# A four-stage transformer block: the second feed-forward with its scales behind the magnitudes, three parts a tile and half-word integers

## The reference

```python
def bit_linear(x, w, g):
    xn = rms_norm(x, g)                       # g: a weight for each column
    scale = 127.0 / clip(max(abs(xn)), 1e-05) # one for each row
    xq = clip(round(xn * scale), -128, 127) / scale
    wq = ...                                  # weights to -1, 0, 1 times one scale
    return xq @ wq.T
y = bit_linear(layernorm(x), gate_w, gate_norm_w)  # 512 -> 2 x 1408
gate, up = split(y, 2)
h = gate * sigmoid(gate) * up
x = x + tanh(g_ffn[1]) * bit_linear(h, down_w, down_norm_w)  # 1408 -> 512
```

## Time and profile before

| | us |
|---|---|
| median of 3 runs (lowest, highest) | 890.92 (889.18, 891.5) |
| the profiled execution | 892.4 |
| its span, first to last instruction | 890.6 |
| TensorE busy | 677.7 (76%) |
| VectorE busy | 681.8 (77%) |
| ScalarE busy | 607.0 (68%) |
| GpSimd busy | 325.4 (37%) |
| granted TensorE clock, mean | 0.90 |
| ScalarE's one table load in `ffn1` (L2106) | 1.28 |
| GpSimd's `integers` over 1408 columns (L2061), mean | 1.44 |

### The profile page before, as it was taken

How to read it: one execution, slowest core, us unless ns; L and a number is a source line. 1 busy time by engine, 2 the same in 40 slices (tenths; PEclk the granted TensorE clock), 3 DMA queues, 4 the chain that set the end, 5 groups by cost and what they waited for, 6 DMA issues and landing times. The chain is left out here.

```text
span 890.6 us, 14235 instructions
## 1 busy us (share of the span) xinstructions
PE 677.7 (76%) x5231; PEld 373.6 (42%) x5262; DVE 681.8 (77%) x1144; ACT 607.0 (68%) x812; POOL 325.4 (37%) x357
## 2 busy tenths in 40 slices
PE   5863367867576856779999988899998377979796
PEld 2431123333233324446555554566455144535453
DVE  1689999999999995886874796556342588989984
ACT  2688698989949883688863885589271155757574
POOL 0113514525685563463561274113031023333233
PEclk9986586998879878689999999999999698989899
DMA  8900300000000002422320121123000000000001
GB/s 317 340 0 0 119 23 1 1 1 1 1 1 1 1 0 99 130 83 70 108 78 1 34 66 45 38 68 106 1 1 1 33 1 12 25 24 24 24 36 48
DMA packets 21760, 43.70 MB, mean 49 GB/s; under 512 B 3904, under 2 KB 8512, under 8 KB 20800
## 3 DMA queue, kind: packets, MB, share of 16 engines
q1 hardware_dynamic: 21696, 42.85, 13.9%
HBM read 38.61 MB, written 4.19 MB: 48 GB/s over the span
## 5 line engine op out<-in xcount | busy, mean ns | idle before, releaser
L1539 DVE TENSOR_REDUCE c_nmax<-c_s 128x1 f32<-128x384 f32 (+3 forms) x176 | 108.6, 633 | 83.3 <-PE c_s L1749 83.3
L1651 ACT ACTIVATE c_probs<-c_e 128x512 f32<-128x512 f32 (+1 forms) x176 | 94.4, 558 | 56.5 <-PE c_e L1779 55.3
L1247 PE MATMUL b_y<-w2q,b_q2T 128*128 128x512 bf16 x254 | 76.6, 457 | 55.7 <-ACT b_q2T L1164 28.1
L1474 POOL TENSOR_TENSOR c_psum<-c_probs 128x1536 f32<-128x1536 f32 x16 | 55.9, 3493 | 155.8 <-ACT c_probs L1651 155.8
L2177 PE MATMUL d_gu<-gateq,d_xqT 128*128 128x352 bf16 x512 | 95.0, 336 | 13.4 <-DVE d_h L1978 12.4
L1746 PE MATMUL c_s<-c_kT,c_qaT 96*128 96x128 f16 (+3 forms) x256 | 73.3, 319 | 22.0 <-DVE c_nmax L1539 19.6
L1777 PE MATMUL c_e<-c_qaT,c_kT 98*128 98x512 f16 (+3 forms) x256 | 69.8, 307 | 4.0 <-ACT c_qaT L1638 3.8
L2106 ACT ACTIVATE d_sg<-d_gu,d_dq 128x352 f32<-128x352 f32 x64 | 35.3, 553 | 54.1 <-PE d_gu L2177 54.1
L1218 PE MATMUL b_up<-shared,b_xqT 128*128 128x512 bf16 x242 | 68.3, 402 | 4.0 <-ACT hidden L1130 2.8
L2177 PEld LDWEIGHTS d_gu<-gateq,d_xqT 128*128 128x128 bf16 x512 | 49.9, 103 | 50.0 <-DVE d_h L1978 18.3
L1247 PEld LDWEIGHTS b_y<-w2q,b_q2T 128*128 128x128 bf16 x256 | 26.5, 111 | 97.1 <-issue 50.0
(11 more groups left out here) (237 smaller groups left out, 1814.6 us busy)
## 6 DMA issues: line engine op xcount, KB each, us to landing
c_stage<-in_gateT SPq DMA_DIRECT2D x16, 704.0 KB, 4.0
c_stage<-in_downT SPq DMA_DIRECT2D x6, 768.0 KB, 4.7
xs<-in_x SPq DMA_DIRECT2D x4, 1024.0 KB, 17.5
a_w1f<-in_w1T SPq DMA_DIRECT2D x2, 2048.0 KB, 16.2
hidden<-in_w2T SPq DMA_DIRECT2D x2, 2048.0 KB, 20.8
out<-xs SPq DMA_DIRECT2D x16, 256.0 KB, 2.0
a_ctxT<-in_ctxT SPq DMA_DIRECT2D x1, 1024.0 KB, 4.9
b_ln_g<-in_ln_g SPq DMA_DIRECT2D x1, 1024.0 KB, 4.8
```

The source lines that it names most:

```text
L1247: last = nc.tensor.matmul(y_ps[:], q2T[:, n % 2, c, :], w2q[:, c, :], start=(c == 0), stop=(c == IC - 1))
L1474: nc.gpsimd.tensor_tensor(psum[:], region(slot, 0)[:, :, P:], region(slot, 1), ALU.add).then_inc(psum_ready, 1)
L1539: nc.vector.tensor_reduce(nmax[:, G % 2, i, n:n + heads], s_ps[u % 2][:, 0:heads * (i + 1) * P].rearrange("p (n k) -> p n k", n=heads), ax ...
L1651: nc.scalar.activation(probs[:, G % 2, at:at + width], e_ps[fill % 3][:, 0:width], ACT.Exp).then_inc(e_read, 1)
```

## The change

- Input quantisation moves to a class `GateInputs`. VectorE centres and weighs the raw tile (`weighted`), takes its maximum (`largest`); the scales are made behind that on GpSimd (`scales`, five operations on one column); ScalarE rounds in place, with the magic number plus 256 (`integers`), so that the low half word of each value is an integer that TensorE transposes as it is. Statistics are taken tile by tile.
- The hidden values go the same way: `weighted` multiplies by `dw` without waiting for the squares, `largest` follows, GpSimd makes all scales in one chain, ScalarE rounds in place; GpSimd's pass over 1408 columns is gone. The copies out of PSUM read 16-bit integers and take 256 off.
- The gate and up columns are in three parts (512, 512, 384) and not four of 352. `u` has three slots, `q2T` two. A tile is turned while tile `n + 2` goes up, and multiplied down in the turn of tile `n + 3`.
- The first two tiles' inputs are made inside `xattn1`: VectorE at units 189 and 190, GpSimd from 189 to 191, ScalarE at 192 and 193. `dw` gets a wait of its own, in front of `weighted(0)`.
- The hardware loops are gone: all 16 tiles are written out on all engines.

Leading parts of the diff; removed functions are those printed above:

```diff
+class GateInputs:
+    SLOTS = 2
...
+        self.bn, self.mv, self.xn = g["prep"].bn, g["prep"].mv, g["prep"].turned
...
+    def weighted(self, dve, n):
...
+        last = self.small.mark(nc.vector.bn_stats(self.bn[:, i, :], self.xs[:, n, :]))
+        dve.wait_ge(self.step, last)
+        last = self.small.mark(nc.vector.bn_aggr(self.mv[:, i, :], self.bn[:, i, :]))
+        dve.wait_ge(self.step, last)
+        nc.vector.tensor_scalar(self.ve[:, c], self.mv[:, i, 1:2], 1.0 + self.EPS, self.EPS * self.EPS,
+                                ALU.mult, ALU.add).then_inc(self.ve_ready, 1)
+        if n >= self.SLOTS:
+            dve.wait_ge(self.xqt_done, n - self.SLOTS + 1)
+        self.small.mark(nc.vector.scalar_tensor_tensor(out=self.xn[:, n % self.SLOTS, :], in0=self.xs[:, n, :], scalar=self.mv[:, i, 0:1],
+                                                       in1=self.gw[:], op0=ALU.subtract, op1=ALU.mult))
+    def largest(self, dve, n):
...
+        self.nc.vector.tensor_reduce(self.mx[:, n:n + 1], self.xn[:, n % self.SLOTS, :], axis=AX, op=ALU.max,
+                                     apply_absolute_value=True).then_inc(self.mx_ready, 1)
+    def scales(self, pool, n):
...
+        last = self.chain.mark(nc.gpsimd.tensor_tensor(self.c1[:, c], self.ve[:, c], self.minus_half[:, 0:1], ALU.pow))
+        pool.wait_ge(self.pstep, last)
+        pool.wait_ge(self.mx_ready, n + 1)
+        last = self.chain.mark(nc.gpsimd.tensor_scalar(self.e[:, c], self.mx[:, c], self.c1[:, c], 1e-5, ALU.mult, ALU.max))
+        pool.wait_ge(self.pstep, last)
+        last = self.chain.mark(nc.gpsimd.tensor_tensor(self.inv[:, c], self.e[:, c], self.minus_one, ALU.pow))
+        self.chain.mark(nc.gpsimd.tensor_scalar(self.dq[:, c], self.e[:, c], self.step_scale, 1.0, ALU.mult, ALU.mult))
+        pool.wait_ge(self.pstep, self.chain.value())
+        nc.gpsimd.tensor_scalar(self.qs[:, c], self.inv[:, c], self.c1[:, c], QMAX, ALU.mult, ALU.mult).then_inc(self.qs_ready, 1)
+    def integers(self, act, n):
...
+        act.wait_ge(self.qs_ready, n + 1)
+        at = self.xn[:, n % self.SLOTS, :]
+        self.nc.scalar.activation(at, at, ACT.Copy, scale=self.qs[:, n:n + 1], bias=MAGIC + LIFT).then_inc(self.rounded, 1)
...
+    INPUTS_AT = UNITS + LAG - 2
...
+                if u == INPUTS_AT:
+                    pool.wait_ge(w_scale_ready, 2)
+                    inputs.setup(pool)
+                if INPUTS_AT < u <= INPUTS_AT + 2:
+                    inputs.scales(pool, u - INPUTS_AT - 1)
...
+                if u == INPUTS_AT:
+                    dve.wait_ge(y_read, 2)
+                    dve.wait_ge(g["vec1_loaded"], 16)
+                if INPUTS_AT <= u < INPUTS_AT + 2:
+                    inputs.weighted(dve, u - INPUTS_AT)
+                    inputs.largest(dve, u - INPUTS_AT)
...
+                if INPUTS_AT + 3 <= u < INPUTS_AT + 5:
+                    inputs.integers(act, u - INPUTS_AT - 3)
...
+    WIDTHS = (DIM, DIM, INTER - 2 * DIM)
...
         def _(dve):
+            for n in range(TOTAL + 3):
+                gated(n, 0)
+                largest(n - 1)
+                gated(n, 1)
+                residual(n - 3)
+                inputs.weighted(dve, n + 2)
+                inputs.largest(dve, n + 2)
+                gated(n, 2)
+                weighted(n)
...
         def _(pool):
+            for n in range(TOTAL + 1):
+                scales(n - 1)
+                inputs.scales(pool, n + 2)
...
         def _(act):
+            gather(0)
+            for n in range(TOTAL + 2):
+                silu(n, 0)
+                if n >= 1:
+                    inputs.integers(act, n + 1)
+                squares(n - 1)
+                silu(n, 1)
+                gather2(n - 2, 0)
+                gather(n + 1)
+                silu(n, 2)
+                gather2(n - 2, 1)
+                integers(n - 1)
...
         def _(pe):
+            turn_inputs(0)
+            for n in range(TOTAL + 3):
+                up(n, 0)
+                down(n - 3)
+                turn_hidden(n - 2, 0)
+                up(n, 1)
+                turn_hidden(n - 2, 1)
+                turn_inputs(n + 1)
+                up(n, 2)
```

More of the change, by code:

```diff
@@ L1972, in gated @@
-            def gated(n, i, k):
+                part = n * PARTS + k
+                if n >= 2 and k == 0:
+                    dve.wait_ge(ssq_ready, n - 1)
+                    dve.wait_ge(u_ready, n - 1)
+                dve.wait_ge(sg_ready, part + 1)
+                nc.vector.scalar_tensor_tensor(out=h[:, n % 2, STARTS[k]:STARTS[k] + WIDTHS[k]], in0=gu_ps[part % 2][:, 1, 0:WIDTHS[k]],
+                                               scalar=inputs.dq[:, n:n + 1], in1=sg[:, part % 2, 0:WIDTHS[k]],
+                                               op0=ALU.mult, op1=ALU.mult).then_inc(h_ready, 1)
@@ L1999, in residual, with _, scales @@
+        @block.gpsimd
+        def _(pool):
+            chain = Tally(pstep)
+            def scales(n):
                 if not valid(n):
                     return
[L2001 to L2020 removed]
@@ L2022, in _ @@
-            nc.vector.memset(minus_one[:], -1.0).then_inc(setup, 1)
-            nc.vector.tensor_scalar(scale2[:], w1_scale[:, 1:2], gate4[:, 3:4], None, ALU.mult).then_inc(setup, 1)
-            dve.wait_ge(vec_loaded, 32)
-            statistics(0)
-            quantise(0, 0, 0)
-            batch(0)
-            with dve.Fori(1, BATCH - 1) as b:
-                small.enter(b - 1, 8 + TILES * 7)
-                batch(b)
-                small.leave(BATCH - 2)
-            batch(BATCH - 1)
@@ L2079, in _ @@
-            pool.wait_ge(setup, 2)
-            inputs_scale(0)
-            batch(0)
-            with pool.Fori(1, BATCH - 1) as b:
-                small.enter(b - 1, TILES * 3)
-                batch(b)
-                small.leave(BATCH - 2)
-            batch(BATCH - 1)
-            batch(BATCH)
-        @block.scalar
-        def _(act):
-            def gather(n, i):
-                if not valid(n):
-                    return
-                act.wait_ge(xqt_done, n + 1)
-                if past(n, 2):
+                act.wait_ge(inputs.xqt_done, n + 1)
@@ L2156, in turn_inputs @@
                 if not valid(n):
                     return
-                pe.wait_ge(xq_ready, n + 1)
-                if past(n, 1):
+                pe.wait_ge(inputs.rounded, n + 1)
+                if n >= 1:
                     pe.wait_ge(xqT_ready, n)
+                rows = low(inputs.xn[:, n % inputs.SLOTS, :])
                 for c in range(CH):
-                    last = nc.tensor.transpose(t1_ps[:, c * P:(c + 1) * P], xq[:, i % 2, c * P:(c + 1) * P], ident_b[:])
-                last.then_inc(xqt_done, 1)
@@ L2165, in up @@
-            def up(n, i, parts):
+                    last = nc.tensor.transpose(t1_ps[:, c * P:(c + 1) * P], rows[:, c * P:(c + 1) * P], ident_b[:])
+                last.then_inc(inputs.xqt_done, 1)
+            def up(n, k):
                 if not valid(n):
                     return
-                if parts[0] == 0:
+                part = n * PARTS + k
+                if k == 0:
                     pe.wait_ge(xqT_ready, n + 1)
-                for k in parts:
-                    part = n * PARTS + k
-                    if not isinstance(part, int) or part >= 2:
-                        pe.wait_ge(h_ready, part - 1)
-                    for half in range(2):
-                        at = half * INTER + k * PART
-                        for c in range(CH):
-                            last = nc.tensor.matmul(gu_ps[k % 2][:, half, 0:PART], xqT[:, i % 2, c, :],
-                                                    gateq[:, c, at:at + PART], start=(c == 0), stop=(c == CH - 1))
-                    last.then_inc(gu_done, 1)
@@ L2181, in turn_hidden @@
-            def turn_hidden(n, i):
+                if part >= 2:
+                    pe.wait_ge(h_ready, part - 1)
+                for half in range(2):
+                    at = half * INTER + STARTS[k]
+                    for c in range(CH):
+                        last = nc.tensor.matmul(gu_ps[part % 2][:, half, 0:WIDTHS[k]], xqT[:, n % 2, c, :],
+                                                gateq[:, c, at:at + WIDTHS[k]], start=(c == 0), stop=(c == CH - 1))
+                last.then_inc(gu_done, 1)
```

324 lines of the change are left out of this document (128 added, 196 removed).

## The result

The changed kernel takes **856.88 us** (median of 4 runs, 856.03 to 858.79) against 890.64 for the kernel before in the same comparison: ratio 0.963, interval 0.960 to 0.965. It gains 33.8 us where 47 were forecast. The profiled execution took 858.79, its span is 856.9.

What follows compares the result with a forecast made beforehand. VectorE was taken to bound the old steady feed-forward, a loop through several engines the new. Span 890.6 + 1.9 (handover) - 12.6 (start) - 27.3 (tiles) - 9.4 (tail) = 843.2, so 843.5 us; range 835 to 857.

Steps and rivals of the forecast that it cites:

- rival B: Second feed-forward: the loop is longer than its parts, 9.3 us a tile, 852 us in all (855 with handover +4); chance 0.18.
- The sign of being wrong: Forecast wrong if tiles over 9 us apart, attention ends after 699, or clock under 0.9 in the middle of the phase.
- the steady tile's 8.5: Second feed-forward, tiles 3 to 13: a loop through VectorE, GpSimd and ScalarE takes 8.5 us a tile, bounds 8.05 and 9.3.
- GpSimd's four operations at 1.8 us: Steady tile's loop: GpSimd's column operations between VectorE's input maximum and ScalarE's input integers, 1.8 us with semaphores and handover.
- The VectorE sum of 8.2: Steady tile: work per engine, VectorE 8.2 us, TensorE 7.9 to 8.05, ScalarE 6.8.
- The handover's +1.9: Attention's end: early inputs delay the last group's `weighed_out` and `attended`, costing 1.9 us, bounds 0 to +4.
- The start, -12.6: Start of the second feed-forward: last residual to first gate falls from 16.7 to 4.1 us, a gain of 12.6.
- The tail: From the last 1408-column product to the end of the span: 12.7 us instead of 22.1, a gain of 9.4.
- the price of nothing: TensorE's new transposes, reading every second half word, cost nothing extra; at double time, 4 us more in all.
- Rival E: Second feed-forward: TensorE's clock falls to 1.2 GHz, 16.1 us a tile, 897 to 965 us in all; chance 0.03.
- C: Second feed-forward: work is better covered, TensorE's 8.05 us decides the tile, 838.5 us in all; chance 0.10.
- D: Attention's end: ScalarE's early wait pushes the attention by as much as the start gains, 854 us in all; chance 0.02.

Runs made afterwards that it cites:

- squares first: The changed kernel with ScalarE's squares put ahead of the input integers in its queue: 843.07 us, ratio 0.9469 to the kernel before.
- both repairs: The changed kernel with the first two tiles' inputs at unit 202, behind the attention, and squares ahead of the input integers: 840.21 us, in a second comparison 840.31.
- the split: The kernel with both repairs, with the product with dw also in two pieces (512 and 896 columns): 841.78 us, ratio 0.9439.
- the spread ones: The changed kernel with VectorE's early inputs behind `attended` of the last two groups and ScalarE's behind its last copy: 855.24 us, ratio 0.9595.

## Why the prediction was right and wrong

What came was the number of rival B, a tile of 9.27 for the 9.3 it names. I gave it 0.18, and 852 (855 with a dear handover); the median lies 2 to 5 us above even that, at the very end of the range, 857. The match is in part luck: the 9.3 is no more than the tile of the kernel before, taken as a bound, and B's reason is late semaphores between full queues, where the runs show one operation of GpSimd held on a loop that the prediction had added up. The sign of being wrong that it named came: tiles more than 9 us apart.

- **The step that failed most is the steady tile's 8.5**, and in it one term: GpSimd's four operations at 1.8 us. They take 2.75. The other terms of the loop were near: ScalarE 2.65 for 2.69, VectorE 3.79 for 3.94 (with the trailing 0.69). I did not ask what VectorE does at the time. It does the new product, which no longer waits for the squares and stands one gate behind the input maximum, so right over GpSimd's chain. The rows of before had a sign of it. The 0.67 of the power is a mean of two lengths, as GpSimd's timeline of the kernel before shows:

```profile
756.97 0.78 POOL L2053 TENSOR_TENSOR d_qs<-d_m,d_minus_one 128x1 f32<-128x1 f32 x1
...
775.44 0.56 POOL L2053 TENSOR_TENSOR d_qs<-d_m,d_minus_one 128x1 f32<-128x1 f32 x1
```

  Seven of its sixteen take 0.78 to 0.84 us, and all seven run beside VectorE's centring of the next inputs (757.18 in the earlier trace rows); the other nine take 0.55 or 0.56, and none of them does. In tiles 3 to 13 the miss is 9.4 us (102.9 for 93.5; two of the eleven tiles took 9.91 and 9.62, which is not explained here), in the last two 1.4 (15.4 for 14.0), in the first three 2.0 (24.8 for 22.8): together the 12.8 of that stretch. With squares first all three shrink to near or under the forecast (92.1, 14.4, 22.3).
- **The VectorE sum of 8.2, TensorE's 7.9 to 8.05 and ScalarE's 6.8 were near as busy times**: 8.03, 8.09, 6.85. As the tile they are too short even with the squares off the loop: it is then 8.31, by TensorE's row and ScalarE's copies behind it, a loop that the prediction did not add up. It had half of the remedy in its hands, since it sets in italics that integers, squares and silu stand in one queue in that order; it took the order as given and priced it.
- **The handover's +1.9 measured +5.0**, outside its bounds of 0 to +4. "The reciprocal is hardly moved" was the wrong step: it moved by 1.90, because the first product was held by GpSimd's sum. The path that it did price was short as well. By the clock of the trace `weighed_out` (678.23) and `attended` (678.84) look earlier than the 680 and 680.5 of the text, but all in front of them ran 2.5 us earlier in this trace (667.15 for 669.67). Counted from that reciprocal the second tile's scale was there after 10.4 us (9.5 in the text), `weighed_out` ran after 11.1 (10.3) and `attended` after 11.7 (10.8), which is 2.76 later than before and not 1.9. The remaining 2.25 is the first projection. The clock, 2.57 in all, was not in the sum: the prediction asked what a rest does to the clock only for the start of the feed-forward.
- **The start, -12.6, was right to the tenth, and so part by part** (4.05 us from last residual to first gate; transposes 0.38, copy 0.60, silu 0.69; TensorE at 1.00), and so was the load of `dw` being hidden. **The tail** was 13.06 for 12.7.
- **Transposes of every second half word are free.** The by-form view of the changed kernel from 741 to 815 us:

```profile
L2198 PE MATMUL d_t<-ident_b,d_u 128*128 128x128 bf16 x88 | 7.5, 219 | 0.0
...
L2170 PE MATMUL d_t<-ident_b,c_turned 128*128 128x128 bf16 x32 | 3.1, 219 | 0.0
```

  219 ns is what packed integers took the earlier trace rows, so the price of nothing stands. The rule that the prediction sets against it is for reads that touch a new line at each access; that every second half word is such a read is shown by no row here, so these rows say nothing for or against that rule.
- **Rival E** had most of its condition: TensorE was busy 8.09 of 9.27 us in short groups, with a rest of 1.13 in each tile. But no group waited that long for a bank: the rest ended with ScalarE's copy of the next inputs (739.91, 749.17). The granted clock stayed at 1.00 from 697 to 856 us. The rule of the Trainium skill, "TensorE: Matmul & The Clock Gate", section A second HAM failure mode: psum-queue depth-cycling, does not bite here.
- **Rivals C and D** did not come. C's 838.5 is near what both repairs give (840.2), and C's limit, TensorE, is then the fullest engine, with 8.15 of 8.31 us for its 8.05; but it took two edits that C does not have.

Left open: what decides on the clock in the first projection. In the six profiles in which TensorE had rested 3.06 us it was slow each time (5.09 to 5.97 us). After rests of 1.17 and 0.94 us it took 3.67 in the kernel before, in both profiles with the two repairs, in that with the split as well, and in that with the inputs behind the attention, but 5.37 without early inputs and with the spread ones, at clocks of 0.56 and 0.71. TensorE's instructions in front are the same and the rests are equal to 0.01 us. After the long rest it fell each time; after the short ones it can go either way, and no run here shows by what. That the rest makes it fall is read from these thirteen profiles; no run changes the rest alone. The kernel before had warned of it in its second feed-forward: behind rests of 5.09, 4.47 and 4.47 us at the ends of three batches the next sixteen multiplications took 4.84 to 4.88 us where eight take 1.36, at a granted clock of 0.63 (740 to 749), 0.58 (783 to 790) and 0.61 (827 to 834). The changed kernel has no such rest there.

## What to carry to other kernels

Price a small GpSimd operation by what VectorE does *at that time*: list for each place on the loop the VectorE instructions beside it, those with two SBUF inputs first (in the kernel before the centring, with one, lengthened a power too). When a loop runs through several in-order queues, ask of each work item in them whether it needs to stand in front of what the loop waits for; here a swap of two neighbours in ScalarE's program was worth 1.4% (853.04 to 840.21, by the ratios of the two kernels with the late inputs). Work moved into a gap of an earlier stage belongs where nothing beside it holds it and nothing urgent stands behind it. The length of the gap did not decide: the 3.56 us in front of the last reciprocal lay over GpSimd's sum and ahead of what TensorE waited for, while the rests in front of the residuals (3.86, then 2.68 us each) took the same work for nothing.

## What the hardware showed that I had not expected

- A GpSimd multiplication of one column, 0.27 us, takes 1.17 when it starts 0.6 us into a VectorE product of 1.62 us with two SBUF inputs, and 0.64 with a product of 1.09: it ends 0.14 us after the product in both. In the attention one takes 0.79 (674.35) beside a product of 0.74 and ends 0.14 after that too. GpSimd's power of one column takes 0.98 beside VectorE's input product and 0.56 elsewhere. It ends 0.41 after that product. A power that started 0.07 us before the long product (743.05) was not lengthened, nor was the product; but seven powers of the kernel before were (0.78 to 0.84 for 0.56), beside VectorE's centring, which reads one tile and not two; six of them had started 0.2 to 0.3 us before it.
- The other way round, GpSimd's addition over 1536 columns held a VectorE product of 0.74 us until 0.55 after its own end, 3.04 in all. VectorE's statistics and small operations of one input ran beside the same sum at their usual length (0.64, 0.18, 0.15).
- Around the end of a rest of 3.06 us TensorE's granted clock was 0.73 (676 to 679 us), and 0.50 in the next 3 us; the five other profiles with such a rest were slow in the same place. After rests of 1.17 and 0.94 us it fell in two profiles of seven; after the rests of 1.1 us in every tile of the feed-forward, between 8 us of work, it stayed at 1.00.
